# Code casts, code fetches and unfinished weight sums given to GpSimd, spreads issued half a step sooner

## The reference

```python
def _dequant(codes, scales):
    w = NF4[codes]
    O, I = w.shape
    w = w.reshape(O, I // BLOCK, BLOCK) * scales[:, :, None]
    return w.reshape(O, I)
...
q = _lin_lora(x, _dequant(codes_attn[0], scales_attn[0]), lora_A_h[0], lora_B_attn[0])
k = _lin_lora(x, _dequant(codes_attn[1], scales_attn[1]), lora_A_h[1], lora_B_attn[1])
v = _lin_lora(x, _dequant(codes_attn[2], scales_attn[2]), lora_A_h[2], lora_B_attn[2])
attn = (q + k + v) / 3.0
o = _lin_lora(attn, _dequant(codes_attn[3], scales_attn[3]), lora_A_h[3], lora_B_attn[3])
x1 = x + o
g = _lin_lora(x1, _dequant(codes_gu[0], scales_gu[0]), lora_A_h[4], lora_B_gu[0])
u = _lin_lora(x1, _dequant(codes_gu[1], scales_gu[1]), lora_A_h[5], lora_B_gu[1])
h = jax.nn.silu(g) * u
d = _lin_lora(h, _dequant(codes_down, scales_down), lora_A_down, lora_B_down)
return x1 + d
```

## Time and profile before

| | |
|---|---|
| runs | 782.98, 783.60, 787.48 us; median 783.6 us |
| the profiled execution | 782.07 us, of which the trace spans 780.7 us |
| granted TensorE clock, mean | 0.967 |
| busy: PE, DVE, ACT, POOL | 705.7, 548.7, 447.7, 219.2 us |

### The profile page before, as it was taken

One profiled execution on the slowest core, in us unless ns is written; L12 is line 12 of the kernel. 1 busy time (PEld: TensorE's weight loads), 2 busy tenths in 40 slices (PEclk: granted clock), 3 DMA queues, 4 the chain that ended last, 5 costly groups with the idle time before them and its releaser, 6 DMA issues.

```text
span 780.7 us, 10711 instructions
## 1 busy us (share of the span) xinstructions
PE 705.7 (90%) x3832; PEld 528.6 (68%) x3832; DVE 548.7 (70%) x1023; ACT 447.7 (57%) x579; POOL 219.2 (28%) x208
## 2 busy tenths in 40 slices
PE   1899766898999999899998999987999999999998
PEld 1565433575777766577775677765777789967886
DVE  6989886656677678898898975657553434587883
ACT  3777768476869587888867511454433121345552
POOL 1004100004265546657676754110401000000000
PEclk9999987899999999999999999989999999969999
DMA  9655578888557678687766212001311101100001
GB/s 351 179 159 197 170 236 254 250 281 256 172 174 245 199 231 256 205 265 239 237 211 195 70 47 70 17 28 42 107 28 48 28 27 42 51 1 13 28 28 41
DMA packets 55542, 110.79 MB, mean 142 GB/s; under 512 B 9905, under 2 KB 20561, under 8 KB 55233
## 3 DMA queue, kind: packets, MB, share of 16 engines
q1 hardware_dynamic: 42912, 80.28, 32.3%
q0 software_dynamic: 4384, 14.09, 6.0%
q10 hardware_dynamic: 8192, 15.73, 5.9%
HBM read 92.19 MB, written 17.89 MB: 141 GB/s over the span
## 4 chain that ended last, share of the span: by engine, by line
PE 46%; DVE 21%; ACT 10%; issue 10%; DMA 8%; SPq 2%; POOL 1%; ACTq 1%; another core or an unknown queue 0%; DVEq 0%; POOLq 0%
PE bank L1248 12%; PE bank L1250 11%; PE bank L1249 11%; ACT hot L1670 3%; DMA rep<-codes 3%; DMA wide_buf<-in_down_flat 2%; DVE x L2032 2%; DVE hot L1919 2%; PE bank L1362 2%; PE bank L1560 2%; DVE bank L1945 1%; ACT c L1630 1%; DVE stats L1840 1%; DVE q_a L1995 1%; DVE q_r L1986 1%
## 5 line engine op out<-in xcount | busy, mean ns | idle before, releaser
L1670 ACT ACTIVATE hot<-rep,levels 128x2048 f16<-128x2048 f16 x94 | 192.9, 2092 | 25.2 <-DMA rep<-codes 15.0
L1248 PE MATMUL bank<-zt_h,w_h 128*128 128x512 f32 (+1 forms) x232 | 93.5, 403 | 2.6 <-DVE zt_l L2020 2.0
L1250 PE MATMUL bank<-zt_h,w_l 128*128 128x512 f32 (+1 forms) x232 | 91.4, 394 | 0.0
L1249 PE MATMUL bank<-zt_l,w_h 128*128 128x512 f32 (+1 forms) x232 | 91.2, 393 | 0.0
L1248 PE MATMUL bank<-w_h,xq_h 128*128 128x512 f32 (+1 forms) x192 | 73.2, 381 | 2.0 <-ACT xq_l L1762 1.6
L1250 PE MATMUL bank<-w_h,xq_l 128*128 128x512 f32 (+1 forms) x192 | 71.2, 371 | 0.0
L1249 PE MATMUL bank<-w_l,xq_h 128*128 128x512 f32 (+1 forms) x192 | 71.2, 371 | 0.0
L1362 PE MATMUL bank<-hot,diag 128*32 128x512 f16 x856 | 61.2, 398 | 7.0 <-ACT hot L1670 4.1
L1919 DVE TENSOR_SCALAR hot<-rep,levels 128x2048 f16<-128x2048 f16 x56 | 54.5, 974 | 4.2 <-DMA rep<-codes 4.1
L1957 DVE TENSOR_TENSOR w_l<-bank,w_h 128x512 fp32r<-128x512 f32 x46 | 31.7, 689 | 32.7 <-ACT w_h L1678 26.7
L2175 POOL TENSOR_TENSOR q_a<-q_a,q_m 128x384 f32<-128x384 f32 (+3 forms) x34 | 36.1, 1060 | 63.9 <-DVE q_m L1804 63.8
(11 more groups left out here) (218 smaller groups left out, 1665.6 us busy)
## 6 DMA issues: line engine op xcount, KB each, us to landing
rep<-codes SPq DMA_DIRECT2D x56, 512.0 KB
codes<-c SPq DMA_DIRECT2D x28, 256.0 KB
raw<-in_codes_gu_t ACTq DMA_DIRECT2D x14, 512.0 KB
sc<-in_scales_gu_t SPq DMA_DIRECT2D x56, 128.0 KB
raw<-in_codes_attn_t ACTq DMA_DIRECT2D x7, 512.0 KB
raw<-in_codes_down_t ACTq DMA_DIRECT2D x7, 512.0 KB
sc<-in_scales_down_t SPq DMA_DIRECT2D x28, 128.0 KB
wide_buf<-in_gate_flat SPq DMA_DIRECT2D x5, 512.0 KB, 5.5
```

What stands on the lines that cost most here:

```text
L1248: PE.matmul(psum, lh, rh, start=first, stop=False, **kw)
L1249: PE.matmul(psum, lh, rl, start=False, stop=False, **kw)
L1250: return PE.matmul(psum, ll, rh, start=False, stop=last, **kw)
L1670: S.activation(hots[plan.slot[hot_ring(t), (t, m)]][:], codes_in_place(t), ACT.Relu, bias=levels[:, at:at + 1], scale=levels[:, at + 1:at ...
```

## The change

Three things. Casts 1 to 8 (`POOL_BATCHES = 9`) and the fetches 2 to 9 are issued by GpSimd instead of ScalarE, the fetches on GpSimd's own DMA queue; casts from 9 on and the other fetches stay. The additions of k's part to the unfinished weight (tiles 2, 3, 8 and 9, `early_merged`) are made by GpSimd; v's stay on VectorE and get a wait for GpSimd's add two tiles before. In `nf4_weights`, ship(i + 2) stands in the same half step as its cast instead of that of the next tile, and spread(t + 3) right behind hits(t + 1) instead of spread(t + 2) at the beginning of the half step, so that a spread stands ahead of the scales' loads of the half step between.

```diff
+POOL_BATCHES = 9
...
     def fetch(i):
         p.add("fetch", i)
-        p.sends("raw_in", ("raw", i))
+        p.sends("raw_pool" if 1 < i <= POOL_BATCHES else "raw_in", ("raw", i))
...
         if not j["fresh"]:
-            p.note("merged", t)
+            p.note("merged" if j["last"] else "early_merged", t)
             if not j["last"]:
-                p.take("q_out", 2, ("z", t), ("dve", "merged", t))
+                p.take("q_out", 2, ("z", t), ("pool", "early_merged", t))
...
             high_parts()
+            if t == 0:
+                spread(CU)
             if u == 0 and i + 2 < len(jobs):
                 cast(i + 2)
                 if i + 3 < len(jobs):
                     fetch(i + 3)
-            if u == 1 and i + 2 < len(jobs):
                 ship(i + 2)
-            spread(t + 2)
             stack_rests()
             if t < tiles:
                 look(t)
@@ -442,6 +443,7 @@
             low_parts()
             if t + 1 < tiles:
                 hits(t + 1)
+                spread(t + 3)
...
+    def cast_done(i):
+
+        if i < POOL_BATCHES:
+            return done("pool", "cast", i)
+        return sem("cast_act"), plan.nth["cast", i] - plan.nth["cast", POOL_BATCHES - 1]
...
-            elif kind == "fetch":
+            elif kind == "fetch" and (key[0] == 1 or key[0] > POOL_BATCHES):
...
-            elif kind == "cast":
+            elif kind == "cast" and key[0] >= POOL_BATCHES:
...
-                if not j["fresh"]:
+                if j["last"] and not j["fresh"]:
                     dve.wait_ge(*done("dve", "scaled", t))
-                    V.tensor_tensor(stays if j["last"] else wsum[u][:], wsum[u][:], into, ALU.add).then_inc(
-                        sem("merged_dve"), 1)
+                    dve.wait_ge(*done("pool", "early_merged", t - CU))
+                    V.tensor_tensor(stays, wsum[u][:], into, ALU.add).then_inc(sem("merged_dve"), 1)
...
+            if kind == "fetch" and 1 < key[0] <= POOL_BATCHES:
+                i, = key
+                pool.wait_ge(*cast_done(i - 1))
+                G.dma_start(raw[:], codes_of(jobs[i]).rearrange("(u p) o -> p u o", p=P)).then_inc(
+                    dma_sem(("raw", i)), 16)
+            elif kind == "cast" and key[0] < POOL_BATCHES:
+                i, = key
+                pool.wait_ge(*landed(("raw", i)))
+                if i > 1:
+                    pool.wait_ge(*landed(("codes", i - 1)))
+                G.tensor_copy(c16[:], raw[:]).then_inc(sem("cast_pool"), 1)
+            elif kind == "assemble" and ("early_merged", *key) in plan.nth:
+                t, = key
+                total = wsum[t % 2][:]
+                pool.wait_ge(*done("dve", "scaled", t))
+                G.tensor_tensor(total, total, q_out[plan.slot["q_out", ("z", t)]][:], ALU.add).then_inc(
+                    sem("early_merged_pool"), 1)
...
-                sp.wait_ge(*done("act", "cast", i))
+                sp.wait_ge(*cast_done(i))
```

More of the change, by code:

```diff
@@ L1262, in phase_ends @@
         weights_end(queue)
-        queue.wait_ge(*done("act", "cast", len(jobs) - 1))
+        queue.wait_ge(*cast_done(len(jobs) - 1))
         for name in ("gate", "up", "down"):
@@ L1618, in act_program @@
                     S.dma_start(x[:, n, :], x_d[:, n, :]).then_inc(dma_sem(("x", n)), 16)
-            elif kind == "fetch":
+            elif kind == "fetch" and (key[0] == 1 or key[0] > POOL_BATCHES):
                 i, = key
                 if i > 1:
-                    act.wait_ge(*done("act", "cast", i - 1))
+                    act.wait_ge(*cast_done(i - 1))
                 S.dma_start(raw[:], codes_of(jobs[i]).rearrange("(u p) o -> p u o", p=P)).then_inc(
                     dma_sem(("raw", i)), 16)
-            elif kind == "cast":
+            elif kind == "cast" and key[0] >= POOL_BATCHES:
                 i, = key
                 act.wait_ge(*landed(("raw", i)))
-                if i > 1:
-                    act.wait_ge(*landed(("codes", i - 1)))
+                act.wait_ge(*landed(("codes", i - 1)))
                 S.copy(c16[:], raw[:]).then_inc(sem("cast_act"), 1)
@@ L2182, in pool_program @@
             kind, key = step[0], step[1:]
-            if kind == "const":
+            if kind == "fetch" and 1 < key[0] <= POOL_BATCHES:
[15 more added lines that the diff above has]
+                    sem("early_merged_pool"), 1)
+            elif kind == "const":
                 pool.wait_ge(*landed("const"))
```

## The result

The changed kernel takes 805.83 us (804.59 to 808.16), where the kernel before took 783.29 us in the same rounds: a ratio of 1.0282, 95% interval 1.0245 to 1.0319, slower by 22.5 us. The forecast was 784, no change. The profiled execution has a span of 803.3 us.

The account below looks back on a forecast made before the run. Casting and spreading were taken to bound before 140 us, SP's loads and reductions to 179. Early gain used up by the loop, + 0.4 + 1.66 - 1.5 gave 0.6 us later than 782.07, forecast as 784 (range 774 to 792).

Parts of the forecast that it names:

- Behind 200 only the sooner spreads remain: After 200 us: sooner spreads shorten TensorE's 4.1 us of waits for ramps by 1.5 us (0 to 4.1).
- The loop of maxima: 140 to 179 us: maxima loads behind waiting spreads take 34.0 us (28.4 to 35.5) from maximum 10 to 16, before 25.9.
- landing: In the loop of maxima: each load right behind a spread takes 6.5 us to land, ends 4.63 and 6.98.
- The early gain: Before 140 us: freed ScalarE and VectorE time brings the first product's merge 7 us earlier (3 to 8).
- ScalarE's time was on the path: Before the merge: from the fifth cast on, four casts taken off ScalarE gain 6.3 us; the first four nothing.
- VectorE's price: Before the merge: GpSimd's new casts and adds slow VectorE by 1 us, with 0 and 4 as ends.
- The queue: SP's queue early: a ship behind its cast holds SP at most 2.3 us per batch, costing nothing without a maxima load behind.
- GpSimd's cast itself: Before 140 us: each 128x1024 cast takes GpSimd 2.3 us, with ScalarE's 1.05 as the other end; time covered.
- The low clock behind the longer wait: TensorE's product near 179 us: waiting some 9 us for zt_l instead of 1.53 brings a low clock costing 1.66 us.
- Rival B: First 80 us: GpSimd and VectorE collide, early gain 3 us or less, loop 35.5 us: 6.8 us slower, 790; chance 0.18.
- Rival A: 140 to 179 us: loads land in 4.63 us, loop 28.4 us, early gain reaches the end: 776 (772 to 778); chance 0.2.

Follow-up runs that it names:

- e3: Changed kernel with the stores of q_d issued by GpSimd itself instead of on SP's queue: 789.50 us.
- e4: Changed kernel with sooner spreads and ships only up to tile 24 (about 190 us), the old places from there: 791.43 us.
- e8: Changed kernel with the stores of q_d and the loads of maxima 10 to 17 issued by GpSimd: 779.35 us, ratio 0.9935 to the kernel before.
- e7: Kernel before, with ScalarE's casts of batches 2 to 8 narrowed to 16 of 512 columns per tile and nothing given to GpSimd: 779.69 us.
- e6: Kernel before with only the eight casts and fetches given to GpSimd; sums, spreads and ships as before: 787.76 us.
- e13: Kernel before with casts and fetches on GpSimd, whose additions of the bias to x take only 16 of 512 columns: 780.20 us.
- e2: Kernel before with only spreads and ships moved; casts, fetches and sums stay on ScalarE and VectorE: 807.11 us.
- e10: Kernel before with sooner spreads and ships, q_d stores and loads of maxima 10 to 17 on GpSimd; casts and sums not moved: 780.49 us.
- e1: Changed kernel with spreads and ships put back where they stood before; casts, fetches and sums stay on GpSimd: 783.89 us.
- e12: Kernel before, with GpSimd copying the f16 codes of batches 1 to 8 once more in place after ScalarE's cast: 785.70 us.

## Why the prediction was wrong

**"Behind 200 only the sooner spreads remain", 1.5 us gained.** This is the step that failed. I walked the spreads past scale loads, ships and loads for the maxima on SP's queue and stopped at 200 us. The same queue carries the stores of q_d there, and each now stood behind a spread that waits for ramps. 17 us, shown by e3 and e4. The gain itself did not come either: TensorE's waits for ramps from 200 to 445 us, 4.1 us in the earlier trace rows, are 9.3 us, and with the stores moved (e3) still 5.3.

**The loop of maxima, 34.0 us.** The mechanism was right, and each step of it can be read in the rows after: 2.9 (3.56) to the ramp, 3.8 (4.34) for the LoRA loads, 1.3 (1.32) for the comparison, 0.6 (0.55) for each spread. The term that was mis-sized is landing: 4.7 to 5.1 us rather than 6.5, which makes 4.8 of the 5.7 us between 34.0 and the 28.4 measured. That this is the low end that was given is luck, as that end has landing at 4.63 and two other steps longer. e8 shows the loop by taking the loads out of it.

**The early gain, 7 us.** 1.8 us late instead. That ScalarE's time was on the path was right (e7: 4.7 us from some 0.8 us for each of seven casts). VectorE's price, 1 us with 4 as the upper end, was the term that was mis-sized: its instructions are 7.8 us longer. I took 0.35 us for a collision from the comparison at 61.97; but that one began when half of the cast was over, and ended 0.54 us behind it. The five new ones cost 0.7 to 1.0 us each. And I left out the additions to x that GpSimd already had: held up behind casts, they now meet other instructions of VectorE (some 3.6 us here; e6 against e13: 6.8 us at the merge). The queue had a share as well, which I put at nothing: with spreads and ships alone the merge begins 2.9 us late in e2, and 1.0 in e10, whose instructions are the same up to there. How the 1.8 us divide is not shown. GpSimd's cast itself, 1.05 us, was cheaper than assumed.

**The low clock behind the longer wait**, 1.66 us: right in size, 1.55 us (13.42 us between the two products, before 11.87), though the wait was 2.46 us and not 9, since merge and zt_l were both late. That the length of the wait decides is not shown: in e1 the wait there was 2.60 us and the granted clock stayed at 1.00.

**Rival B** had the early half: no gain left by what GpSimd and VectorE do to each other. But its loop of 35.5 us did not come, so that its 6.8 us are near the 5.1 at 191 by luck, and they are not the 22.6 at the end. **Rival A**'s landing came true and its gain did not, as the early gain it needs wasn't there. That with the sum of errors the range (774 to 792) missed by 14 us is due to the first step alone: 805.8 less 17 is 789. That the rest would have lain in the range is partly luck: the early gain came out 8.8 us worse than forecast and the loop 5.7 us better.

What stays open: e8 and e10 lose 3 us of their lead again between 385 and 450 us and e13 falls back by 2 us there, and no run tells why.

## What to carry to other kernels

When an issue is moved on an in-order DMA queue, list everything that shares the queue until the end of the program, not only where the move is felt first: a store that frees a buffer is as urgent as a load. An instruction that waits should stand last among those that are ready; if it must be early, move the ready ones to another queue, as the maxima's loads here. On a shared engine count for a new instruction not only its own length but also what it holds up behind its wait, and what that then meets.

## What the runs showed of the hardware that was not expected

GpSimd casts 128x1024 int32 to f16 in 1.05 us (median; 1.04 to 1.50), as fast as ScalarE (1.05). VectorE's comparison beside GpSimd's work is not slowed in proportion but held to the end of it, through three additions in a row (4.07 us for 0.82): in the rows at 48.30, 99.45 and, of e6 and e12, 82.33 and 82.30 it ends 0.55 to 0.57 us behind GpSimd. The Trainium skill (SBUF — State Buffer, section SBUF: two separate sides) states that one of the two holds the shared port pair for a whole instruction while the other waits; these rows agree. The Trainium skill's other warning there, that VectorE keeps GpSimd from writing the descriptors of a DMA which GpSimd issues, shows in the issue: that of 27.51 us lasts 1.56 us, until 29.07, 0.14 us behind a comparison of VectorE (27.59 to 28.93), that of 58.68 1.06 us, until 59.74, 0.15 us behind one that ends at 59.59, where the shortest take 0.72. In the time to landing it doesn't show; the fetches, KB each and median us from issue to landing, from ScalarE's queue and from GpSimd's in the changed kernel:

```profile
raw<-in_codes_gu_t ACTq DMA_DIRECT2D x12, 512.0 KB, 5.1
...
raw<-in_codes_attn_t POOLq DMA_DIRECT2D x6, 512.0 KB, 4.6
...
raw<-in_codes_gu_t POOLq DMA_DIRECT2D x2, 512.0 KB, 5.0
```

They land in 4.6 and 5.0 us, no later than ScalarE's 5.1, though at other times of the run; what they cost is 0.72 to 1.56 us of GpSimd for each issue, where ScalarE took 0.37 to 0.46.
